# Fp32 value products, and four of six probability blocks turned by transfers and VectorE with one more step of lag, in a transformer block kernel

## The chip, the cores and the metric

The kernel runs on one core of a Trainium2 chip. The core has a matmul engine (TensorE, PE in the rows; its weight loads are PEld), VectorE (DVE), ScalarE (ACT), GpSimd (POOL), a queue engine that issues transfers (SyncE, SP), and 16 DMA engines. The metric is the device time of one execution in microseconds (us). Lower is better.

## The reference

One transformer block is applied to 16 sequences of 256 tokens with 256 channels. Attention has 16 heads of 128 dimensions; all heads share one key and one value projection, and each head scales them per token:

```python
q = (x @ Wq.T).reshape(b, n, H, D)
...
k = jnp.einsum('bnd,bnh->bnhd', kp, kh)
v = jnp.einsum('bnd,bnh->bnhd', vp, vh)
q = rope(q)
k = rope(k)
...
scores = jnp.where(mask[None, None], scores, -jnp.inf)
p = jax.nn.softmax(scores, axis=-1)
o = jnp.einsum('bhnm,bmhd->bnhd', p, v).reshape(b, n, H * D)
return o @ Wout.T
```

The mask is causal. kh and vh come from decayed running sums over the tokens. Layer norms, residual sums and a gated feed-forward part with ternary weights follow. Everything is fp32.

## The kernel before

The attention part handles two heads of one sequence, a pair, at a time: 8 pairs a sequence and 128 pairs in all, numbered g. It is a software pipeline written out by hand. In a step s every engine does one stage of several pairs, in the order written in that engine's `batch` function, and `LAG` says how many steps behind its projection a pair reaches each stage: score 1, softmax 2, turn 3, value 4, out 5. Engines meet only through semaphores. An engine works strictly in its written order, so an instruction that waits holds up all that stands behind it on that engine.

The steps of a pair are:

- TensorE projects its queries (`project`, products of high and low parts: three matmuls for each product). VectorE multiplies by cosines (`queries_cos`), ScalarE swaps halves (`swap`), GpSimd multiplies by sines and adds (`queries_sin`, `queries_add`, lines 616 and 626), and also scales the keys (`scale_keys`, line 639).
- TensorE makes the scores (`score`, lines 950 and 952, plain fp32). For the later 128 queries there are 256 keys, for the earlier 128 queries there are 128: 384 columns, three blocks of 128 x 128 a head, six a pair. VectorE masks them into the SBUF buffer T and finds the maxima (`maxima`, lines 1629 and 1631), ScalarE takes the exponentials (`exponent`), VectorE inverts the sums (`invert_sums`, line 1641), and GpSimd multiplies by the inverses (`normalise`, line 650).
- TensorE turns the six blocks by matmuls with the identity (`turn`, lines 967 to 969). ScalarE scales them by vh and writes the high parts, VectorE the low parts (`split_pt`, line 1654). TensorE multiplies them with the values in three passes (`value`, line 798 with pt_split), and later with Wout (`project_out`, line 798 with wo_hi and wo_lo).

T has two buffers, used by pairs in turn. Once in eight steps there is work for the next sequence (`front_at`) and for the last one (`tail_at`): projections of keys and values, layer norm, the residual sum. In some steps a chunk of the feed-forward weights is made ternary (`weights_...`, VectorE on bf16 tensors in SBUF). SyncE loads the scales of the keys two steps ahead, and moves blocks of 32 columns onto 32 partitions so that VectorE's transpose, which turns squares of 32 x 32, can complete the turn of the next sequence's x (`spread_blocks`, line 490, and `turn_x`, line 1514). The feed-forward part starts in the last steps of attention (`FSTART`, `UNIT0`) and goes on for 16 units.

## Time and profile before

| | |
|---|---|
| time, median of 3 runs | 1030.47 us (1030.17 to 1030.52) |
| profiled execution, its own time | 1030.4 us |
| its span in the profile | 1028.4 us |
| busy: PE, PEld, DVE, ACT, POOL | 1014.0, 975.8, 837.9, 861.1, 911.7 us |
| DMA | 64.19 MB, 62 GB/s in the mean |

The profile is one execution on the chip, taken by the hardware profiler. The span runs from its first instruction to its last; 2.0 us of the execution's own time lie outside. Busy time is the time in which an engine had an instruction under way. Matmuls overlap, so a matmul's duration is longer than the time until the next one starts, and rates are read from the starts.

### The profile page before, as it was taken

To read this page: it belongs to the slowest core of one execution; us is meant where nothing else is said; L and a number is where in the kernel's file an instruction comes from. 1 tells how busy PE (TensorE), PEld (TensorE's weight loads), DVE (VectorE), ACT (ScalarE), POOL (GpSimd) and SP (SyncE) were. 2 spreads that over 40 slices of the span, in tenths; PEclk is the share of its full clock that TensorE was granted. 3 is DMA by queue.
4 is the path that set the end of the run, shared out by engine and by line. 5 is a ranking of instruction groups with operands and counts; after the bars stand their busy time and mean duration, and the time that the engine had idled before them with its cause. 6 is when DMAs were issued, how large, how long until landed. Compare 5 with 4: busy or idle time off the path is not lost. (4 is left out here: it accounts for less than half of the span.)

```text
span 1028.4 us, 25055 instructions
## 1 busy us (share of the span) xinstructions
PE 1014.0 (99%) x7777; PEld 975.8 (95%) x7777; DVE 837.9 (81%) x2871; ACT 861.1 (84%) x2427; POOL 911.7 (89%) x848
## 2 busy tenths in 40 slices
PE   7999999999999999999999999999999999999997
PEld 6899999999999999999999999999999999999997
DVE  6978888888888898889888889887777766677776
ACT  5988888988898989898989898889898867877774
POOL 4888999999999999999999999999899847877786
PEclk9999999999999999999999999999999999999999
DMA  7561121112111211221122112111130000000001
GB/s 255 204 196 48 52 69 52 48 62 69 52 51 61 75 51 53 66 75 48 43 73 78 47 54 77 54 47 64 47 114 33 1 2 12 22 22 28 27 21 42
DMA packets 45587, 64.19 MB, mean 62 GB/s; under 512 B 4512, under 2 KB 26464, under 8 KB 45152
## 3 DMA queue, kind: packets, MB, share of 16 engines
q1 hardware_dynamic: 45456, 62.60, 19.5%
q8 instruction: 62, 1.02, 0.4%
q14 instruction: 69, 0.57, 0.2%
HBM read 50.92 MB, written 9.18 MB: 58 GB/s over the span
## 5 line engine op out<-in xcount | busy, mean ns | idle before, releaser
L650 POOL TENSOR_TENSOR arena<-arena 128x768 f32<-128x768 f32 x128 | 195.9, 1530 | 14.2 <-DVE arena L1641 13.9
L626 POOL TENSOR_TENSOR arena<-arena 128x512 f32<-128x512 f32 x128 | 180.3, 1408 | 10.0
L616 POOL TENSOR_TENSOR arena<-arena,tables 128x512 f32<-128x512 f32 x128 | 165.3, 1292 | 20.0 <-ACT arena L1269 19.3
L1654 DVE SCALAR_TENSOR_TENSOR pt_split<-psum,vh_col,pt_split 128x256 fp32r<-128x256 f32 (+1 forms) x512 | 176.8, 406 | 3.5 <-ACT pt_split L1299 3.4
L639 POOL TENSOR_TENSOR arena<-arena 128x512 f32<-128x512 f32 x127 | 163.3, 1286 | 0.0
L1280 ACT ACTIVATE arena<-arena 128x256 f32<-128x256 f32 x256 | 128.3, 501 | 40.7 <-DVE arena L1631 36.1
L950 PE MATMUL psum<-arena 128*128 128x256 f32 x512 | 153.6, 382 | 3.1 <-POOL arena L626 1.9
L798 PE MATMUL psum<-wo_hi,o_hi 128*128 128x256 f32 x512 | 152.0, 297 | 0.0
L798 PE MATMUL psum<-xt_lo,wq_hi 128*128 128x256 f32 x512 | 144.5, 282 | 0.0
L798 PE MATMUL psum<-xt_hi,wq_lo 128*128 128x256 f32 x512 | 144.4, 282 | 0.0
L798 PE MATMUL psum<-wo_hi,o_lo 128*128 128x256 f32 x512 | 144.2, 282 | 0.0
L798 PE MATMUL psum<-xt_hi,wq_hi 128*128 128x256 f32 x512 | 144.0, 281 | 0.0
L798 PE MATMUL psum<-wo_lo,o_hi 128*128 128x256 f32 x512 | 143.6, 281 | 0.0
L798 PE MATMUL psum<-pt_split,vals_hi 128*128 128x512 f32 (+1 forms) x512 | 142.1, 359 | 0.1
L1038 PE MATMUL psum<-xt_hi,wq_hi 128*128 128x256 f32 x512 | 125.6, 282 | 0.0
L1038 PE MATMUL psum<-xt_lo,wq_hi 128*128 128x256 f32 x512 | 124.4, 284 | 0.0
L1298 ACT ACTIVATE pt_split<-psum,vh_col 128x256 fp32r<-128x256 f32 x256 | 120.6, 471 | 0.4 <-PE psum L969 0.4
L1268 ACT ACTIVATE arena<-psum 64x512 f32<-64x512 f32 x128 | 76.1, 595 | 45.0 <-DVE arena L1616 43.6
L952 PEld LDWEIGHTS psum<-arena 128*128 128x128 f32 x512 | 97.2, 190 | 13.3
L1629 DVE CUSTOM_DVE_ANT_0 arena<-psum,mask 128x256 f32<-128x256 f32 x256 | 106.7, 417 | 0.0
L1663 DVE TENSOR_TENSOR o_lo<-psum,o_hi 128x512 fp32r<-128x512 f32 x128 | 87.1, 680 | 23.6 <-ACT o_hi L1308 23.0
L1282 ACT ACTIVATE arena<-arena 128x128 f32<-128x128 f32 x256 | 99.3, 388 | 0.0
(202 smaller groups left out, 3378.1 us busy)
## 6 DMA issues: line engine op xcount, KB each, us to landing
arena<-kh_rows SPq DMA_DIRECT2D x127, 256.0 KB, 3.4
out<-spare SPq DMA_DIRECT2D x15, 256.0 KB, 2.1
moved<-arena SPq DMA_DIRECT2D x56, 64.0 KB, 2.2
arena<-w_rows SPq DMA_DIRECT2D x6, 512.0 KB, 4.8
X<-L_attn_Wout SPq DMA_DIRECT2D x1, 2048.0 KB, 15.0
X<-L_attn_x SPq DMA_DIRECT2D x1, 2048.0 KB, 9.9
arena<-arena SPq DMA_DIRECT2D x30, 64.0 KB, 2.0
arena<-L_attn_Wq SPq DMA_DIRECT2D x1, 1536.0 KB, 10.6
```

Source lines behind the costliest of these rows:

```text
L616: nc.gpsimd.tensor_tensor(swap, swap, spread, ALU.mult).then_inc(q_sined, 1)
L626: nc.gpsimd.tensor_tensor(q_rot[p % 2], q_cos[p % 2], q_swap[p % 2], ALU.add).then_inc(q_roped, 1)
L639: nc.gpsimd.tensor_tensor(k_head[p % 2], keys[par].unsqueeze(1).to_broadcast([P, HP, N]), kh_all[p % 4], ALU.mult).then_inc(k_scaled, 1)
L650: nc.gpsimd.tensor_tensor(tb, tb, r.unsqueeze(3).to_broadcast([P, HP, 3, P]), ALU.mult).then_inc(p_ready, 1)
L798: last = nc.tensor.matmul(o, a, b, start=start and i == 0, stop=stop and i == len(passes) - 1, skip_group_check=skip)
L950: nc.tensor.matmul(sj[:, 0:2 * P], q[:, j, P:N], kt[:, j, :], start=True, stop=True, skip_group_check=True)
L1038: last = nc.tensor.matmul(bank[c % 2 * 2 + half][:, j * N:(j + 1) * N], wgu_t[:, k, col:col + P], part[:, k, :], start=n == 0 and j == 0, ...
L1280: nc.scalar.activation(tb[:, j, 0:2 * P], tb[:, j, 0:2 * P], ACT.Exp, scale=-1.0, bias=nmax[p % 4][:, 2 * j:2 * j + 1], accum_out=rsum[p % ...
L1282: nc.scalar.activation(tb[:, j, 2 * P:3 * P], tb[:, j, 2 * P:3 * P], ACT.Exp, scale=-1.0, bias=nmax[p % 4][:, 2 * j + 1:2 * j + 2], accum_ ...
L1298: nc.scalar.activation(pt_hi[p % 2][:, j * N:(j + 1) * N], b[:, 0:N], ACT.Copy, scale=vh[:, 0, h:h + 1])
L1629: nc.vector.tensor_tensor_reduce(tb[:, j, 0:2 * P], S_BANK[j][:, 0:2 * P], mask[:, :], -1.0, -MASKED, ALU.add, ALU.min, nmax[p % 4][:, 2 * ...
L1654: last = nc.vector.scalar_tensor_tensor(pt_lo[p % 2][:, o], b[:, i], vh[:, t, h:h + 1], pt_hi[p % 2][:, o].bitcast(F32), ALU.mult, ALU.sub ...
```

## The change

The value products become plain fp32 (two matmuls a pair in place of six), so ScalarE writes the scaled probabilities once, as fp32, and VectorE's low parts go away, as do the low parts of the values. Of the six blocks, TensorE turns only the two of the earlier queries. The four of the later queries are kept in T in another column order (`T_rows`, with the keys of `score` read in that order), moved by four transfers of 64 KB a pair from SyncE (`exchange`), and turned in squares of 32 x 32 by VectorE into the same PSUM banks (`fill_pt`, first in VectorE's step). The stages turn, value and out come one step later, T has three buffers, and the stages of the tail and the start of the feed-forward part are one step later too. `normalise` multiplies 12 groups of 64 columns in place of 6 groups of 128, with inverses written by two reciprocals.

```diff
-LAG = dict(project=0, cos=0, swap=0, key=0, rope=1, score=1, softmax=2, turn=3, value=4, out=5)
+LAG = dict(project=0, cos=0, swap=0, key=0, rope=1, score=1, softmax=2, turn=4, value=5, out=6)
...
-TAIL = dict(copy=5, stats=7, invert=9, norm_a=11, norm_b=12, add=14)
+TAIL = dict(copy=6, stats=8, invert=10, norm_a=12, norm_b=13, add=15)
...
-FSTART = PAIRS + 1
+FSTART = PAIRS + 2
...
+        T_rows = lambda g, j: T[g % 3][:, 0:4 * P].rearrange("p (b j r) -> p b j r", j=HP, r=P // 2)[:, :, j, :]
+        T_early = lambda g, j: T[g % 3][:, (4 + j) * P:(5 + j) * P]
...
+            def exchange(g0, s):
+
+                at = pair_at(g0, s, LAG["softmax"])
+                if at:
+                    g = at[0]
+                    sp.wait_ge(p_ready, g + 1)
+                    at_least(sp, pt_filled, (g - 2) * HP + HP)
+                    for b in range(4):
+                        sp.dma_start(blocks[g % 2][b * 32:(b + 1) * 32, :].rearrange("q (a e) -> q a e", e=P),
+                                     T[g % 3][:, b * P:(b + 1) * P]).then_inc(p_exchanged[g % 2], 16)
...
-                    nc.gpsimd.tensor_tensor(tb, tb, r.unsqueeze(3).to_broadcast([P, HP, 3, P]), ALU.mult).then_inc(p_ready, 1)
+                    nc.gpsimd.tensor_tensor(tb, tb, rinv[p % 4][:, 0:12].unsqueeze(2).to_broadcast([P, 12, P // 2]), ALU.mult)\
+                        .then_inc(p_ready, 1)
...
-                        nc.tensor.matmul(sj[:, 0:2 * P], q[:, j, P:N], kt[:, j, :], start=True, stop=True,
+                        by_blocks = kt[:, j, :].rearrange("p (m b c) -> p b m c", m=NT, b=4)
+                        nc.tensor.matmul(sj[:, 0:2 * P], q[:, j, P:N], by_blocks, start=True, stop=True,
...
-                        b = PT_BANK[j]
-                        at_least(pe, pt_lo_done, head_count(g - 1, j))
-                        nc.tensor.transpose(b[:, 0:P], tb[:, j, 2 * P:3 * P], ident[:, :])
-                        nc.tensor.transpose(b[:, P:2 * P], tb[:, j, 0:P], ident[:, :])
-                        nc.tensor.transpose(b[:, 2 * P:3 * P], tb[:, j, P:2 * P], ident[:, :]).then_inc(pt_ready, 1)
+                        at_least(pe, pt_done, head_count(g - 1, j))
+                        nc.tensor.transpose(PT_BANK[j][:, 0:P], T_early(g, j), ident[:, :]).then_inc(pt_ready, 1)
...
-                    three_passes(O_BANK, [(vh[:, 0, :], vl[:, 0, :], ph[:, first], pl[:, first])], stop=False, skip=True)
-                    three_passes(heads(O_BANK, N)[:, :, P:N], [(vh[:, 1, :], vl[:, 1, :], ph[:, second], pl[:, second])],
-                                 start=False, skip=True).then_inc(o_ready, 1)
+                    nc.tensor.matmul(O_BANK, v[:, 0, :], pv[:, first], start=True, stop=False, skip_group_check=True)
+                    nc.tensor.matmul(heads(O_BANK, N)[:, :, P:N], v[:, 1, :], pv[:, second], start=False, stop=True,
+                                     skip_group_check=True).then_inc(o_ready, 1)
...
-                        act.wait_ge(pt_ready, head_count(g, j))
+                        act.wait_ge(pt_filled, head_count(g, j))
...
-            def split_pt(g0, par, s, j):
+            def fill_pt(g0, s):
 
                 at = pair_at(g0, s, LAG["turn"])
                 if at:
...
+                    g, p, _ = at
+                    dve.wait_ge(p_exchanged[g % 2], g // 2 * 64 + 64)
+                    for j in range(HP):
+                        dve.wait_ge(pt_ready, head_count(g, j))
+                        nc.vector.transpose(PT_BANK[j][:, P:3 * P].rearrange("p (m q a) -> p m a q", m=NT, a=4),
+                                            blocks[g % 2][:, :].rearrange("p (a j m c) -> p j m a c", j=HP, m=NT, c=32)[:, j])\
+                          .then_inc(pt_filled, 1)
```

The order of TensorE's instructions shows turn and value of one step, between the end of `project_out` and the next `project`. Before, from the second head's turn on:

```order
L967 MATMUL psum<-ident,arena 128x128
L968 MATMUL psum<-ident,arena 128x128
L969 MATMUL psum<-ident,arena 128x128
L798 MATMUL psum<-pt_split,vals_hi 128x512 x2
L798 MATMUL psum<-pt_split,vals_lo 128x512
L798 MATMUL psum<-pt_split,vals_hi 128x2x128 x2
L798 MATMUL psum<-pt_split,vals_lo 128x2x128
L798 MATMUL psum<-xt_hi,wq_hi 128x256
```

After the change, both heads' turns and the value products of the same place:

```order
L817 MATMUL psum<-wo_hi,o_lo 128x256
L985 MATMUL psum<-ident,arena 128x128 x2
L1000 MATMUL psum<-pt,vals 128x512
L1001 MATMUL psum<-pt,vals 128x2x128
L817 MATMUL psum<-xt_hi,wq_hi 128x256
```

Six turns became two, and six value matmuls became two, one of 512 and one of 256 columns.

VectorE's order at the fifth step of a sequence (`L1556` or `L1572` are the decays of the next sequence, `BN_STATS` its statistics). Before:

```order
L1631 ISA arena 128x1
L1556 RECIPROCAL psum<-arena 32x128
L1641 RECIPROCAL arena<-arena 128x8
L1500 BN_STATS arena<-X 128x6
L1505 BN_AGGR arena<-arena 128x2 x2
L1663 TENSOR_TENSOR o_lo<-psum,o_hi 128x512
L1616 TENSOR_TENSOR arena<-psum,tables 128x512
L1654 SCALAR_TENSOR_TENSOR pt_split<-psum,vh_col,pt_split 128x256
L1654 SCALAR_TENSOR_TENSOR pt_split<-psum,vh_col,pt_split 128x128
```

After the change:

```order
L1642 ISA arena 128x1
L1666 STREAM_TRANSPOSE psum<-blocks 128x2x4x32 x2
L1572 RECIPROCAL psum<-arena 32x128
L1653 RECIPROCAL inverses<-arena 128x8
L1655 RECIPROCAL inverses<-arena 128x4
L1516 BN_STATS arena<-X 128x6
L1521 BN_AGGR arena<-arena 128x2 x2
L1675 TENSOR_TENSOR o_lo<-psum,o_hi 128x512
L1625 TENSOR_TENSOR arena<-psum,tables 128x512
L1639 MEMSET arena 128x1
```

The four low parts (L1654) behind the cosines are gone, and two transposes stand ahead of everything else in the step.

SyncE's order around the same sequence's last steps, before and after:

```order
L483 DMA arena<-kh_rows 128x512 x2
L490 DMA moved<-arena 32x4x128 x4
L535 DMA w_tern_t<-arena 128x512
L483 DMA arena<-kh_rows 128x512 x4
```

```order
L499 DMA blocks<-T_third 32x4x128 x4
L488 DMA arena<-kh_rows 128x512
L506 DMA moved<-arena 32x4x128 x4
L551 DMA w_tern_t<-arena 128x512
L499 DMA blocks<-arena 32x4x128 x4
L488 DMA arena<-kh_rows 128x512
```

Between any two loads of key scales (L483, now L488) there are now four transfers of blocks (L499), which wait for `normalise`.

## Rows read from the trace of the kernel before

**Rows 1.** The page, part 1: busy us and share of the span

```profile
PE 1014.0 (99%) x7777; PEld 975.8 (95%) x7777; DVE 837.9 (81%) x2871; ACT 861.1 (84%) x2427; POOL 911.7 (89%) x848
```

**Rows 2.** Windows: stretch, length, busy us (instructions) per engine, granted clock, DMA share, GB/s

```profile
412.00:512.00 100.00, 100.00 (x757) 95.81 (x755) 87.62 (x320) 88.45 (x269) 95.39 (x80) 1.00 0.19 60
712.00:805.00 93.00, 93.00 (x706) 89.27 (x705) 70.85 (x284) 81.46 (x245) 85.14 (x72) 1.00 0.19 62
```

**Rows 3.** Timeline of PE in one step: start us, duration us, engine, line, operation

```profile
500.72 0.27 PE L967 MATMUL psum<-ident,arena 128*128 128x128 f32 x1
...
501.26 0.27 PE L969 MATMUL psum<-ident,arena 128*128 128x128 f32 x1
...
502.43 0.28 PE L798 MATMUL psum<-xt_hi,wq_hi 128*128 128x256 f32 x1
...
503.87 0.59 PE L950 MATMUL psum<-arena 128*128 128x256 f32 x2
...
504.52 0.38 PE L950 MATMUL psum<-arena 128*128 128x256 f32 x1
```

**Rows 4.** Timeline of PE: the first turn in two steps that follow each other

```profile
432.57 0.27 PE L967 MATMUL psum<-ident,arena 128*128 128x128 f32 x1
...
438.44 0.27 PE L967 MATMUL psum<-ident,arena 128*128 128x128 f32 x1
```

**Rows 5.** Timeline of POOL in three steps

```profile
413.61 1.27 POOL L616 TENSOR_TENSOR arena<-arena,tables 128x512 f32<-128x512 f32 x1
...
418.88 1.30 POOL L616 TENSOR_TENSOR arena<-arena,tables 128x512 f32<-128x512 f32 x1
...
421.62 2.35 POOL L650 TENSOR_TENSOR arena<-arena 128x768 f32<-128x768 f32 x1
...
429.65 1.47 POOL L650 TENSOR_TENSOR arena<-arena 128x768 f32<-128x768 f32 x1
```

**Rows 6.** Groups of POOL, 413 to 513.2: busy us, mean ns | idle before, releaser

```profile
L650 POOL TENSOR_TENSOR arena<-arena 128x768 f32<-128x768 f32 x16 | 24.8, 1552 | 1.2 <-DVE arena L1641 1.2
...
L616 POOL TENSOR_TENSOR arena<-arena,tables 128x512 f32<-128x512 f32 x16 | 20.6, 1286 | 1.3 <-ACT arena L1269 1.3
...
L607 POOL TENSOR_TENSOR X<-X,arena 128x512 f32<-128x512 f32 x2 | 2.6, 1288 | 0.0
```

**Rows 7.** Timelines of DVE and POOL at two places

```profile
421.46 1.18 DVE L1688 TENSOR_TENSOR arena<-arena 128x1024 bf16<-128x1024 bf16 x1
...
714.08 0.73 DVE L1514 STREAM_TRANSPOSE psum<-moved 128x512 f32<-128x512 f32 x1
714.34 1.29 POOL L626 TENSOR_TENSOR arena<-arena 128x512 f32<-128x512 f32 x1
```

**Rows 8.** Timeline from one pair's scores to the next pair's

```profile
435.71 0.59 PE L950 MATMUL psum<-arena 128*128 128x256 f32 x2
...
437.24 0.59 ACT L1269 ACTIVATE arena<-psum 64x512 f32<-64x512 f32 x1
...
438.56 0.51 ACT L1280 ACTIVATE arena<-arena 128x256 f32<-128x256 f32 x1
...
439.27 1.29 POOL L626 TENSOR_TENSOR arena<-arena 128x512 f32<-128x512 f32 x1
...
440.46 0.20 DVE L1641 RECIPROCAL arena<-arena 128x8 f32<-128x8 f32 x1 [0.56 <-ACT arena L1282]
...
441.61 0.38 PE L950 MATMUL psum<-arena 128*128 128x256 f32 x1
```

**Rows 9.** Groups of DVE, whole span, columns as in rows 6

```profile
L1654 DVE SCALAR_TENSOR_TENSOR pt_split<-psum,vh_col,pt_split 128x256 fp32r<-128x256 f32 (+1 forms) x512 | 176.8, 406 | 3.5 <-ACT pt_split L1299 3.4
```

**Rows 10.** SyncE's timeline: four issues of 64 KB, merged

```profile
407.11 2.54 SPq L490 DMA_DIRECT2D moved<-arena  x4
```

**Rows 11.** The tile `moved`: its 56 transfers of 64 KB each

```profile
DMA to landing us min/median/max: 2.2/2.2/3.9
```

**Rows 12.** Waits of PE, whole span: waiting line, releaser, us, times, longest

```profile
PE psum L950 <- POOL arena L626: 1.9, 3, 0.9
```

More of the change, by code:

```diff
@@ L54 @@
 FRONT = dict(move=-1, turn=0, split=0, split_lo=1, keys=1, gates=2, gates_one=2, key_cos=3, key_swap=3, key_rope=4,
-             decay_a=3, decay_b=4, coef=5, weigh=5, sum=5, store=6, made=5, taken=5, turned=6, values_hi=7, values_lo=7, vh=7)
+             decay_a=3, decay_b=4, coef=5, weigh=5, sum=5, store=6, made=5, taken=5, turned=6, values_copy=7, vh=7)
 AHEAD = dict(stats_a=3, stats_b=4, invert=5, norm_a=6, norm_b=6, move=7)
@@ L67 @@
 FLEAD = 8
-UNIT0 = dict(stats=-4, invert=-3, norm_a=-2, norm_b=-1, turn=0, split=0, split_lo=1, up=PAIRS + 1, multiply=PAIRS + 2)
-FSTART = PAIRS + 1
+UNIT0 = dict(stats=-4, invert=-3, norm_a=-2, norm_b=-1, turn=0, split=0, split_lo=1, up=PAIRS + 2, multiply=PAIRS + 3)
+FSTART = PAIRS + 2
 FC = 2
@@ L110, in sandwich_kernel @@
         moved = sb("moved", [P, NT * E])
+        blocks = [sb(f"blocks{i}", [P, 4 * P]) for i in range(2)]
+        inverses = sb("inverses", [P, 64])
+        T_third = sb("T_third", [P, HP * 3 * P])
         cosq, sinq, cosk, sink = (tables[:, i, :] for i in range(4))
@@ L115, in sandwich_kernel @@
         xt_lo = [sb(f"xt_lo{i}", [P, ET, N], F32R) for i in range(2)]
-        vals_hi = [sb(f"vals_hi{i}", [P, NT, D], F32R) for i in range(2)]
-        vals_lo = [sb(f"vals_lo{i}", [P, NT, D], F32R) for i in range(2)]
+        vals = [sb(f"vals{i}", [P, NT, D]) for i in range(2)]
         vh_col = [sb(f"vh_col{i}", [P, NT, 2 * H]) for i in range(2)]
@@ L125, in sandwich_kernel @@
         spare = sb("spare", [P, 2 * NT * E])
-        pt_split = sb("pt_split", [P, 2, 2, 6 * P], F32R)
-        pt_hi, pt_lo = ([pt_split[:, j, i, :] for i in range(2)] for j in range(2))
+        pt_all = sb("pt", [P, 2, 6 * P])
+        pt = [pt_all[:, i, :] for i in range(2)]
         arena = sb("arena", [P, ARENA])
@@ L148, in sandwich_kernel @@
         T_at = used[0]
-        T = [carve(HP, 3 * P) for _ in range(2)]
+        T = [carve(HP * 3 * P) for _ in range(2)] + [T_third[:, :]]
         k_head = [carve(HP, N) for _ in range(2)]
@@ L210, in sandwich_kernel @@
         rsum = [small[:, 16 + 4 * i:20 + 4 * i] for i in range(4)]
-        rinv = [small[:, 96 + 8 * i:104 + 8 * i] for i in range(4)]
+        rinv = [inverses[:, 16 * i:16 * i + 16] for i in range(4)]
         ln1_stat = small[:, 48:60].rearrange("p (t a) -> p t a", a=6)
@@ L535, in batch @@
                         sp.dma_start(rows.rearrange("(p f) -> p f", f=FF // 2), w_turned_bf).then_inc(wt_stored, 16)
+                    exchange(g0, s)
             store_kh(0, 0)
@@ L1640, in invert_sums @@
                     dve.wait_ge(p_exp, head_count(g, HP - 1))
-                    nc.vector.reciprocal(heads(rinv[p % 4], 2), rsum[p % 4].unsqueeze(2).to_broadcast([P, 2 * HP, 2]))\
-                        .then_inc(p_inv, 1)
-            def split_pt(g0, par, s, j):
+                    sums, made = rsum[p % 4].rearrange("p (j t) -> p t j", t=NT), rinv[p % 4]
+                    nc.vector.reciprocal(made[:, 0:8].rearrange("p (b j) -> p b j", j=HP),
+                                         sums[:, 0, :].unsqueeze(1).to_broadcast([P, 4, HP]))
+                    nc.vector.reciprocal(made[:, 8:12].rearrange("p (j h) -> p j h", j=HP),
+                                         sums[:, 1, :].unsqueeze(2).to_broadcast([P, HP, 2])).then_inc(p_inv, 1)
+            def fill_pt(g0, s):
                 at = pair_at(g0, s, LAG["turn"])
                 if at:
-                    g, p, back = at
-                    vh, h, b = vh_col[par ^ back], H + p * HP + j, PT_BANK[j]
-                    dve.wait_ge(pt_hi_done, head_count(g, j))
-                    at_least(dve, o_ready, g - 1)
-                    for t, (o, i) in enumerate(((slice(j * N, (j + 1) * N), slice(0, N)),
-                                                (slice(HP * N + j * P, HP * N + (j + 1) * P), slice(N, N + P)))):
-                        last = nc.vector.scalar_tensor_tensor(pt_lo[p % 2][:, o], b[:, i], vh[:, t, h:h + 1],
-                                                              pt_hi[p % 2][:, o].bitcast(F32), ALU.mult, ALU.subtract)
-                    last.then_inc(pt_lo_done, 1)
+                    g, p, _ = at
[5 more added lines that the diff above has]
+                          .then_inc(pt_filled, 1)
             def split_o(g0, s):
@@ L1934, in batch @@
                         queries_cos(g0, s)
-                    for j in range(HP):
-                        split_pt(g0, par, s, j)
                     if g0 == STEPS:
```

93 lines of the change are left out of this document (44 added, 49 removed).

## The prediction

> **What bounds the kernel now.** I read the busy times first. TensorE is busy for 99% of the span, GpSimd for 89% [rows 1]. The windows place this: between 412 and 512 us TensorE has no idle time and its weight loads are busy for 95.8 of 100 us, at a granted clock of 1.00, and GpSimd is busy for 95.4 [rows 2]. So in attention, which is some 780 us of the span, TensorE ends everything last. From 712 us, when the ternary chunks are done, GpSimd has 85.1 of 93. The list of waits agrees: TensorE waited for GpSimd's add for only 1.9 us in all [rows 12].
>
> How near GpSimd is decides this case. A regular step is 5.87 us long on TensorE [rows 4], and GpSimd's four instructions of a step repeat after 5.27 (413.61 to 418.88) [rows 5]. The other steps are longer on both, and 16 steps, two sequences, take 100.2 us, the length of the window that rows 6 come from. In these 16 steps GpSimd waited for another engine for 1.2 us ahead of `normalise` and 1.3 ahead of the sines [rows 6]. It therefore needs about 100.2 - 2.5 = 97.7 us for its own work. That is all the room there is below TensorE.
>
> Part of this need is not work. At 421.62 `normalise` took 2.35 us in place of 1.47 [rows 5], while VectorE ran a bf16 comparison with two inputs in SBUF from 421.46 on for 1.18 [rows 7]. There are six such VectorE instructions in 16 steps, as long as chunks are made.
>
> **The change part by part.**
>
> Turns: the first starts at 500.72, the sixth at 501.26, so they follow at 0.11 us each [rows 3], though each lasts 0.27. Four fewer: 4 x 0.11 = 0.44 us a step less.
>
> Here a rule is weighed that would change the term. The Trainium skill ("TensorE: Matmul & The Clock Gate", PE-mode transpose) gives about 275 ns for a transpose of 128 x 128 inside a kernel. The trace has the same 0.27 us as a duration, but not as the distance of starts. By the page's figure the term would be about 1.1 us; by the starts it is 0.44.
>
> Values: before, from the end of the last turn (501.26 + 0.11) to the first projection at 502.43 are 1.06 us [rows 3]. Plain fp32 is in the scores: from 503.87 to 504.52 are 0.65 us for 256 + 128 columns [rows 3], 1.69 ns a column. 768 columns give 1.30 us, 0.24 more. A column of fp32 in the scores costs the same in both sizes, so I take this as it is, with 0.05 us either way.
>
> TensorE's step becomes 5.87 - 0.44 + 0.24 = 5.67, by 0.20 shorter with rounding; I use 0.19. If only TensorE mattered: 128 x 0.19 = 24.3 us less.
>
> VectorE: it loses 4 x 0.406 us of low parts a step [rows 9] and gets two transposes and a second reciprocal. The transpose of 512 columns took 0.73 [rows 7]; half of it costs between 0.37 and about 0.45 if part is fixed, so 0.9 for two, plus 0.20 [rows 8]: 1.1 against 1.62. Hidden, and VectorE gets freer. The transposes now stand first in its step and wait for TensorE's turns; queued behind them are `invert_sums`, the weights' work, and what GpSimd needs of them. In rows 8 the scores start at 435.71 and the next turns at 438.44 [rows 4], 2.73 later. The transposes would end about 2.73 + 0.2 + 0.9 = 3.85 after the scores' start. The exponentials of the pair started at 438.56 and the sums were inverted at 440.46, 1.90 later [rows 8]. Without the low parts ahead of the maxima they can start when the swap is done at 437.83, 2.12 after the scores' start, so they end at about 4.05. The add of GpSimd, ahead of `normalise`, ends at 440.56, 4.85 after [rows 8]. So the transposes are covered by 0.2 us at one point and a microsecond at the other. Without the cover, each late 0.1 us would first eat into that microsecond.
>
> Do the new transposes hold up GpSimd, as the bf16 comparison did? At 714.08 the existing one ran for 0.73 beside the add of 714.34, which took its usual 1.29 [rows 7]. I cost it at nothing.
>
> Transfers: four issues take SyncE 2.54 us [rows 10], and with one landing in 2.2 us the last arrives 1.9 + 2.2 = 4.1 us after `normalise`; at the longest landing of 3.9 [rows 11] it is 5.8. `normalise` at 429.65 ended at 431.12 [rows 5] and its turn started at 432.57 [rows 4]: 1.45. With one step more of lag the room is 1.45 + 5.68 = 7.1. Hidden by 1.3 to 3.0. SyncE issues for 2.54 + about 0.4 of 6.1 us, and the key scales, loaded two steps ahead, stand behind.
>
> `normalise`: the same 768 columns in 12 groups. Below: nothing. Above: 768 columns in six groups take 1.47 [rows 5], 512 columns in two groups 1.29 [rows 6]; if the 256 further columns were free, the groups would cost 0.18, and twice as many 0.18 again. But 256 columns are not free at 1.29 for 512, so I take 0.
>
> What GpSimd gives back. While chunks are made (96 of 128 steps), TensorE would want 100.2 - 16 x 0.19 = 97.2 us for 16 steps and GpSimd 97.7. The slack that evens this out is short: the add ends at 440.56, the scores that need it start at 441.61 [rows 8], 1.05 us; with the shorter step it is 0.86. I carried GpSimd's lag from step to step through 16 steps, with its extra work in the steps where the new `TAIL` puts it. The residual sum of 1.29 [rows 6] moves from the seventh to the eighth step, where the weights' scales also stand. It reaches 1.2 us three times, and TensorE waits 0.8 to 1.6 us in 16 steps. I take 1.2, times 6 = 7.2. As GpSimd no longer idles, VectorE's bf16 instructions hit it more fully. The one in rows 5 cost it 0.88. Over 16 steps `normalise` lost 16 x (1.552 - 1.47) = 1.3 us to them [rows 6], so by far not all six cost as much today. I add 0.5 for 16 steps, 3.0, as an estimate between 0 and 2 a period. In the other 32 steps it needs its 85.1 plus some 2 of gaps of its own (estimate, 97.7 - 95.4 for 16 steps in the busier stretch), 87.2, against 93 - 15 x 0.19 = 90.1: no wait.
>
> Start and drain: one more step of turn, value and out (0.22 + 1.30 + 1.43 = 2.95 us of TensorE) moves from the filling of the pipeline, where TensorE has idle time, to its emptying, where pairs now pass through transfers and VectorE too. I take 2.0, between 0 and 4.
>
> Sum on the profiled execution: 1030.4 - 24.3 + 7.2 + 3.0 + 2.0 = 1018.3. It lies at the median of the runs, 1030.47, so 1018 for the median. The forecast is faster by 12 us, half of what TensorE saves, GpSimd the new bound for three quarters of attention.
>
> **The rivals.**
>
> Full gain: GpSimd's collisions and waits are absorbed, since VectorE is freer and delivers its sums earlier. For it: VectorE's load falls by half a microsecond a step. Against it: the 97.7 us. It gives 1030.4 - 24.3 + 2 to 5 = 1008 to 1011. Chance 0.12.
>
> GpSimd dearer, which ends on the other side: `normalise` over 12 groups costs more, or collisions come in full. Place: the 96 steps with 97.7 of 97.2 us, where each 0.1 us goes wholly into the time, 9.6 us, and less in the other 32 with their 0.2 us of room a step. It decides from about 0.12 us a step. At the upper bound of 0.18 it gives 1018 + 96 x 0.18 = 1035, and 1037 with some waits in the other 32. For it: no row has this shape. Against: the price by column. Chance 0.25, with 0.06 still faster, 0.06 the same and 0.13 slower.
>
> Here the Trainium skill ("SBUF — State Buffer", Who interferes with whom) states that a VectorE instruction with two SBUF inputs and a reading GpSimd instruction exclude each other for the whole instruction. Rows 5 and 7 agree: 0.88 us more beside an instruction of 1.18. By the rule in full, each of the six would cost 1.18, 0.3 more than here: 1.8 in 16 steps, 11 us in all, 1026 in place of the 1018 that counts 3.0 of it.
>
> Late blocks: the exchange takes over 7.1 us, VectorE stands at the head of its step, and its sums, low parts and cosines are late with it. For it: SyncE waits in order for chunk stores and layer norms. Against: 4.1 to 5.8. With 7.5 us, 0.4 a step: 1018 + 128 x 0.4 less the overlap with GpSimd's waits, about 1050. Chance 0.05.
>
> Dear turns: the distance of starts understates what four turns cost, and TensorE's step falls by 1.1 - 0.24. Then GpSimd alone bounds: 6 x (100.2 - 97.7) + 2 x (93.0 - 87.2) = 27 us, and with 2 for start and drain 1005. It is what the page's figure would do. Chance 0.02.
>
> **How the numbers follow.** Forecast 0.56 for 1011 to 1025. With the others: faster by over 0.2% (about what a measurement of this kernel can tell from no change) 0.56 + 0.12 + 0.06 + 0.02 = 0.76, the same 0.06, slower 0.13 + 0.05 = 0.18. The range of 1008 to 1033 leaves out half of the full gain's low side, the dear turns, and the slower cases beyond a few microseconds, 0.2 together.
>
> **What the next profile would show.** TensorE's turn to first projection 1.52 us apart, down from 1.71. Regular steps of 5.68. `normalise` at 1.47 when undisturbed. GpSimd's idle ahead of `normalise` and the sines near zero between 412 and 512, and TensorE waiting 1 to 2 us for the add in 16 steps. 16 steps in 98 to 99 us. VectorE's transposes at 0.37 to 0.45, with waits for TensorE but none for transfers, and landings of 2.2. The prediction is wrong if `normalise` is longer, if VectorE waits for the transfers, or if the scores' rate changes with the new order of the keys, which I cost at nothing.

## The result and the profile after

The changed kernel takes 1044.81 us (median of 4 runs, 1042.77 to 1046.26) against 1030.32 us (1030.13 to 1030.52) before on the same chip. The ratio is 1.0139, 95% interval 1.0125 to 1.0154. It is slower by 14.5 us, where 12 us less were forecast. The profiled execution took 1044.94 us and its span is 1042.8, so here too some 2 us lie outside.

The page of the changed kernel, part 1, answers to [rows 1]:

```profile
PE 1003.8 (96%) x7009; PEld 906.7 (87%) x7009; DVE 759.0 (73%) x2727; ACT 855.5 (82%) x2427; POOL 903.3 (87%) x849
```

TensorE lost 10 us of busy time and the span gained 14, so it now has idle time that it did not have. The windows say the same, against [rows 2]:

```profile
412.00:512.00 100.00, 96.83 (x639) 85.23 (x638) 74.48 (x288) 84.72 (x262) 91.53 (x77) 0.98 0.33 98
712.00:805.00 93.00, 92.85 (x623) 81.69 (x622) 63.94 (x271) 83.32 (x257) 87.54 (x75) 1.00 0.39 113
```

The row to look at is GpSimd's: 91.5 of 100 us where it was 95.4. The prediction said that GpSimd would become the bound, and it is idler than before. Something has to be late for it. Rows from the list of waits of the changed kernel (waiting line, releaser, us, times, longest):

```profile
DVE psum L1666 <- PE psum L985: 111.3, 122, 2.7
ACT arena L1284 <- DVE arena L1625: 75.6, 91, 3.8
PEld psum L970 <- POOL arena L645: 32.1, 35, 2.4
POOL arena L668 <- DVE inverses L1655: 29.3, 34, 3.4
...
PE psum L970 <- POOL arena L645: 24.0, 20, 2.2
...
POOL T_third L668 <- DVE inverses L1655: 11.3, 14, 1.4
...
DVE psum L1666 <- DMA blocks<-T_third: 4.4, 1, 4.4
```

TensorE's wait for GpSimd's add was 1.9 us [rows 12] and is 24.0. VectorE now stands for 111.3 us at the head of its step, waiting for TensorE's turns; ScalarE's swap waits 75.6 us for the cosines. GpSimd waits for the inverses for 29.3 and 11.3 us (two rows, by T's buffer), where it was 13.9 before. For transfers there is a single wait of 4.4 us, so they are hidden, as was said.

**Where the time went.** I took the start of each pair's first score matmul from TensorE's timelines and cut the span with it: the first 16 steps with what is ahead of them, the 96 steps with chunks of weights, the last 15 steps, and from the last pair's scores to the end. In us:

| | before | after | change | predicted |
|---|---|---|---|---|
| to the scores of pair 16 | 121.6 | 122.0 | +0.4 | -3.0 |
| 96 steps | 601.4 | 612.0 | +10.6 | -8.0 |
| last 15 steps | 91.4 | 89.7 | -1.7 | -2.9 |
| from the last scores on | 214.0 | 219.0 | +5.0 | +2.0 |
| span | 1028.4 | 1042.8 | +14.4 | -11.9 |

The column "predicted" splits the prediction's sum: 0.19 us less a step everywhere, +7.2 and +3.0 in the 96 steps, +2.0 for start and drain put in the last row, and the last pair's own 0.2 left out. So 18.6 of the 26 us of error are in the 96 steps.

**What happens there.** The waits of GpSimd alone in the 96 steps, before and then after:

```profile
POOL arena L616 <- ACT arena L1269: 8.7, 26, 0.7
POOL arena L650 <- DVE arena L1641: 6.9, 25, 0.6
```

```profile
POOL arena L668 <- DVE inverses L1655: 20.4, 26, 1.4
POOL T_third L668 <- DVE inverses L1655: 9.2, 12, 1.4
POOL arena L635 <- ACT arena L1285: 4.3, 12, 0.5
```

GpSimd was idle for 15.6 us in them and is now for 33.9, and the added time is nearly all ahead of `normalise` (29.6 us in place of 6.9). There are 38 such waits. In 21 of them, 19.5 us together, the exponentials had ended 1.3 to 3.0 us before the inversion started, and the inversion was queued on VectorE behind the transposes and the work that follows them. In the other 17, 10.0 us, the inversion waited for the exponentials on ScalarE. Steps are counted from a sequence's first, in twos of sequences. The first kind stands in the second, third, ninth and eleventh of 16 steps, the second in the eighth and the last two. In the kernel before the inversion came 0.03 us after the exponentials' end in most steps, and 0.8 at most in the mean of a step's place. Here is the first kind, in a second step of 16:

```profile
427.27 0.19 ACT L1298 ACTIVATION_READ_ACCUMULATOR arena<-arena 128x1 f32 x1
...
427.85 0.79 DVE L1666 STREAM_TRANSPOSE psum<-blocks 128x256 f32<-128x256 f32 x2 [1.42 <-PE psum L985]
428.55 0.67 DVE L1534 TENSOR_TENSOR xt_lo<-psum,xt_hi 128x512 fp32r<-128x512 f32 x1
429.14 0.17 DVE L1653 RECIPROCAL inverses<-arena 128x8 f32<-128x8 f32 x1
...
429.44 2.36 POOL L668 TENSOR_TENSOR arena<-arena,inverses 128x768 f32<-128x768 f32 x1 [1.22 <-DVE inverses L1655]
```

The longest waits of TensorE, 1.8 us, come behind the last of 16 steps. Its rows, from the timelines of PE, DVE, ACT and POOL of the changed kernel (start, duration, engine, line, operation):

```profile
412.14 0.79 DVE L1666 STREAM_TRANSPOSE psum<-blocks 128x256 f32<-128x256 f32 x2 [0.24 <-PE psum L985]
...
413.03 0.49 ACT L1296 ACTIVATE arena<-arena 128x256 f32<-128x256 f32 x1
...
414.78 0.70 PE L970 MATMUL psum<-arena 128*128 128x256 f32 x2
...
414.91 0.20 DVE L1653 RECIPROCAL inverses<-arena 128x8 f32<-128x8 f32 x1 [1.99 <-ACT arena L1298]
...
415.05 0.57 ACT L1324 ACTIVATE o_hi<-psum 128x512 fp32r<-128x512 f32 x1
...
415.23 1.47 POOL L668 TENSOR_TENSOR arena<-arena,inverses 128x768 f32<-128x768 f32 x1 [0.51 <-DVE inverses L1655]
...
415.65 0.69 DVE L1675 TENSOR_TENSOR o_lo<-psum,o_hi 128x512 fp32r<-128x512 f32 x1
...
416.26 0.68 DVE L1625 TENSOR_TENSOR arena<-psum,tables 128x512 f32<-128x512 f32 x1
...
417.92 1.28 POOL L626 TENSOR_TENSOR X<-X,arena 128x512 f32<-128x512 f32 x1
419.29 0.27 POOL L676 TENSOR_SCALAR arena<-arena 128x16 bf16<-128x16 f32 x1
...
420.34 1.28 POOL L635 TENSOR_TENSOR arena<-arena,tables 128x512 f32<-128x512 f32 x1
421.70 1.27 POOL L645 TENSOR_TENSOR arena<-arena 128x512 f32<-128x512 f32 x1
...
423.02 1.02 PE L970 MATMUL psum<-arena 128*128 128x256 f32 x2 [1.81 <-POOL arena L645]
```

Two things meet. The cosines (L1625) start 1.48 us after the scores' start, though TensorE has their input ready by then. In the kernel before they start 0.20 us after it in 11 of the 16 steps that I laid side by side, and never later than 0.8. At this place the transposes are not what holds them: they ended at 412.93, and VectorE then stood for 1.99 us until ScalarE had the exponentials. ScalarE had been busy with the swap, held up by the cosines of the step before (410.09), with a layer norm, and with the exponentials, and it writes the high part of o (L1324) behind them, for which the low part (L1675) and the cosines wait. So a late cosine comes back one step later through ScalarE as late sums and a late cosine. The second thing is GpSimd's queue: after waits of 0.69, 0.50 and 0.51 us in three instructions it is busy without a pause from 415.23 to 422.97, with the residual sum (L626) and the weights' scales (L676 to 679) in one step. The sines (L635) start 2.16 us after the swap's end at 418.18, and TensorE idles for 1.81. In the eighth step of the 16 there is a second such place with 1.2 us of idle time.

### The profile page after: what moved, and what is told of

Read it like the earlier page. It is cut to its first block and busy times, and to the rows that moved or that the text cites. A ratio compares the mean times of both kernels' runs of the same rounds, so it can differ in the third digit from the quotient of the medians.

```text
span 1042.8 us, 23874 instructions
## 1 busy us (share of the span) xinstructions
PE 1003.8 (96%) x7009; PEld 906.7 (87%) x7009; DVE 759.0 (73%) x2727; ACT 855.5 (82%) x2427; POOL 903.3 (87%) x849
## 5 line engine op out<-in xcount | busy, mean ns | idle before, releaser
L970 PE MATMUL psum<-arena 128*128 128x256 f32 x512 | 160.6, 396 | 25.6 <-POOL arena L645 24.0
L1666 DVE STREAM_TRANSPOSE psum<-blocks 128x256 f32<-128x256 f32 x256 | 100.7, 439 | 115.7 <-PE psum L985 111.3
L645 POOL TENSOR_TENSOR arena<-arena 128x512 f32<-128x512 f32 x128 | 171.3, 1338 | 10.0
L635 POOL TENSOR_TENSOR arena<-arena,tables 128x512 f32<-128x512 f32 x128 | 164.4, 1284 | 10.0 <-ACT arena L1285 9.1
L817 PE MATMUL psum<-xt_hi,wq_hi 128*128 128x256 f32 x512 | 167.8, 328 | 0.2 <-ACT arena L1285 0.2
L658 POOL TENSOR_TENSOR arena<-arena 128x512 f32<-128x512 f32 x127 | 163.6, 1289 | 0.0
L668 POOL TENSOR_TENSOR arena<-arena,inverses 128x768 f32<-128x768 f32 x86 | 132.2, 1538 | 29.9 <-DVE inverses L1655 29.3
L1284 ACT ACTIVATE arena<-psum 64x512 f32<-64x512 f32 x128 | 76.2, 595 | 79.9 <-DVE arena L1625 75.6
L1000 PE MATMUL psum<-pt,vals 128*128 128x512 f32 x256 | 131.2, 594 | 1.5 <-DVE o_lo L1675 1.5
L1054 PE MATMUL psum<-xt_hi,wq_hi 128*128 128x256 f32 x512 | 125.6, 282 | 0.0
L1314 ACT ACTIVATE pt<-psum,vh_col 128x256 f32<-128x256 f32 x256 | 120.3, 470 | 4.2 <-DVE psum L1666 4.2
L972 PEld LDWEIGHTS psum<-arena 128*128 128x128 f32 x512 | 98.8, 193 | 14.1
L970 PEld LDWEIGHTS psum<-arena 128*128 128x128 f32 x512 | 78.3, 192 | 34.3 <-POOL arena L645 32.1
L1675 DVE TENSOR_TENSOR o_lo<-psum,o_hi 128x512 fp32r<-128x512 f32 x128 | 86.6, 676 | 27.9 <-ACT o_hi L1324 26.0
L1001 PEld LDWEIGHTS psum<-pt,vals 128*128 128x128 f32 x256 | 48.6, 190 | 61.2 <-issue 61.2
L817 PEld LDWEIGHTS psum<-xt_hi,wq_hi 128*128 128x128 f32 x512 | 96.5, 188 | 4.2 <-issue 0.9
## 6 DMA issues: line engine op xcount, KB each, us to landing
X<-L_attn_x SPq DMA_DIRECT2D x1, 2048.0 KB, 11.3
```

The lines of the kernel that those rows point to most:

```text
L635: nc.gpsimd.tensor_tensor(swap, swap, spread, ALU.mult).then_inc(q_sined, 1)
L645: nc.gpsimd.tensor_tensor(q_rot[p % 2], q_cos[p % 2], q_swap[p % 2], ALU.add).then_inc(q_roped, 1)
L658: nc.gpsimd.tensor_tensor(k_head[p % 2], keys[par].unsqueeze(1).to_broadcast([P, HP, N]), kh_all[p % 4], ALU.mult).then_inc(k_scaled, 1)
L668: nc.gpsimd.tensor_tensor(tb, tb, rinv[p % 4][:, 0:12].unsqueeze(2).to_broadcast([P, 12, P // 2]), ALU.mult)\
L817: last = nc.tensor.matmul(o, a, b, start=start and i == 0, stop=stop and i == len(passes) - 1, skip_group_check=skip)
L970: nc.tensor.matmul(sj[:, 0:2 * P], q[:, j, P:N], by_blocks, start=True, stop=True, skip_group_check=True)
```

## The experiments

In the expectations, theory A is that the inverses of the sums come late and hold up `normalise`; theory B that the bunching of residual sum and scales costs the time; theory D that the cosines come late on VectorE; C and E are told in the expectations themselves. Every kernel is compared with the kernel before. The mean of the six 16-step stretches of the 96 steps, from the timelines, stands beside each: it is 100.2 us before and 102.0 after.

**fill_late.** The two transposes go behind the inversion of the sums.

```diff
-                    fill_pt(g0, s)
...
                     invert_sums(g0, s)
+                    fill_pt(g0, s)
```

> The changed kernel with VectorE's transposes of a step behind the inversion of the sums instead of first in the step. Theory A (the transposes wait for TensorE's turns at the head of VectorE's step, the inverses are late behind them, and GpSimd, which has no room, stands idle ahead of normalise for 5.8 us in 16 steps): GpSimd's idle there falls to about 1 us, 16 steps fall from 103.1 to 99 or 100 us, and the time to 1020 to 1027. Theory B (the residual sum and the weights' scales now meet in one step and only that stalls TensorE): the time stays within 3 us of 1044.8. Theory C (transfers and SyncE's longer queue slow the steps): no change either.

Measured: 1051.29 us (1050.88 to 1053.34), ratio 1.0208 (1.0191 to 1.0225), 6.5 us more than the change, and 16 steps in 102.9. Its waits:

```profile
DVE inverses L1653 <- ACT arena L1298: 98.6, 74, 3.0
...
POOL arena L635 <- ACT arena L1285: 30.6, 44, 4.3
ACT pt L1314 <- DVE psum L1666: 25.7, 39, 4.2
...
POOL arena L668 <- DVE inverses L1655: 12.2, 18, 1.7
```

GpSimd's wait for the inverses fell from 29.3 to 12.2 us and the time still grew, so the 1020 to 1027 of theory A fail. VectorE now stands waiting for the sums of the exponentials, and what is behind, transposes and cosines, is later still: ScalarE's write of pt waits 25.7 us for the transposes, and the sines 30.6 for the swap. It doesn't show that late inverses are harmless. In the 96 steps GpSimd's waits for them fall from 29.6 to 12.6 us and those for the swap rise from 4.3 to 18.6: this edit moves the idle time from one path to the other.

**add14.** The residual sum goes back to the seventh step.

```diff
-TAIL = dict(copy=6, stats=8, invert=10, norm_a=12, norm_b=13, add=15)
+TAIL = dict(copy=6, stats=8, invert=10, norm_a=12, norm_b=13, add=14)
```

> The changed kernel with the residual sum one step earlier (TAIL add=14), so that it does not meet the weights' scales. Theory B: the wait of TensorE of some 2 us in the last step of every second sequence goes, with the clock's drop behind it, 10 to 13 us in all: 1032 to 1035. Theory A: GpSimd still idles ahead of normalise, and only some of that wait goes: 1038 to 1043. Theory C: no change.

Measured: 1034.99 us (1032.17 to 1035.58), 1.0041 (1.0027 to 1.0055), 9.8 us less than the change, 16 steps in 100.0. Theory B holds: one digit is worth 9.8 us. In the 96 steps no wait of TensorE for the add is over 1.0 us any more.

**fill_late_add14.** Both edits together.

> Both edits. Theory A with B as a smaller second part: 1016 to 1022, what the sum of the prediction said. If either alone gives all, this equals that one within 2 us.

Measured: 1046.31 us (1045.48 to 1047.12), 1.0157 (1.0140 to 1.0174), 16 steps in 101.9, where 1016 to 1022 was expected: a miss, for the reason seen in fill_late. The late transposes cost 11.3 us beside add14, more than the 6.5 beside the change: with the bunched step out of the way less of them lies under another wait, as I read it.

**turn_early.** TensorE makes the two turns right behind the scores of the step before, so that VectorE finds them done. (In the fourth step of the first sequence, where a later turn of weights uses the place, they come at the step's end.)

```diff
-                    turn(g0, par, s)
                     value(g0, par, s)
...
                     score(g0, par, s)
...
+                    else:
+                        turn(g0, par, s + 1)
...
+                    if is_first(g0, s - 3):
+                        turn(g0, par, s + 1)
```

> The changed kernel with VectorE's order as it is, but TensorE's two turns of a pair right behind the scores of the step before, ahead of the next sequence's work and the output products. Theory A in its narrow form (what costs is the wait for the turn, not the 0.9 us that the transposes take at the head of the step): as good as fill_late or better, 1018 to 1027, and VectorE's wait for the turns of 111 us goes below 30. If the transposes' own time ahead of the inverses costs: 1030 to 1038. Theories B and C: within 3 us of 1044.8.

Measured: 1036.72 us (1035.59 to 1037.80), 1.0061 (1.0044 to 1.0078), 8.1 us less than the change, 16 steps in 100.6. The row of VectorE's 111.3 us of waits for the turns is gone from the list, and GpSimd's waits for the inverses in the 96 steps fall from 29.6 to 10.5 us. So the path through the inverses does cost. The 1018 to 1027 for the wait alone failed; the run lies in the 1030 to 1038 that was expected if the transposes' own time costs too.

**fill_small.** Each transpose turns a single square of 32 columns in place of 256; most of the turning is left out.

```diff
-                        nc.vector.transpose(PT_BANK[j][:, P:3 * P].rearrange("p (m q a) -> p m a q", m=NT, a=4),
-                                            blocks[g % 2][:, :].rearrange("p (a j m c) -> p j m a c", j=HP, m=NT, c=32)[:, j])\
+                        nc.vector.transpose(PT_BANK[j][:, P:P + 32], blocks[g % 2][:, j * 32:(j + 1) * 32])\
```

> The changed kernel, in which each of VectorE's two transposes of a pair turns one square column of 32 instead of all 256 columns, at the same place and with the same waits. It leaves out most of the turning, so the probabilities of the later queries are not right. Theory D, formed after the first four runs (the cosines of the queries come late, because the transposes, the inversion and the low part of the output all have to pass through VectorE between TensorE's turns and the end of its projection, and the sines, the add and the scores are late behind them): the transposes' own 0.9 us falls to some 0.4, cosines start 0.2 us after the scores' start in most steps again, and the time falls by 8 to 14 us to 1031 to 1037. If only the wait for the turns mattered: within 3 us of 1044.8.

Measured: 1037.57 us (1037.08 to 1038.67), 1.0069 (1.0052 to 1.0086), 7.2 us less, 16 steps in 101.3. The transposes' own length costs about as much as their wait for the turns, though only 4.3 of the 7.2 us are in the 96 steps and 2.0 are up to pair 16. Neither is hidden.

**cos_first.** On VectorE the cosines go ahead of the low part of o. Two calls change places.

```diff
-                    if g0 < STEPS:
-                        split_o(g0, s)
                     if not (is_first(g0, s) or is_first(g0, s - 2) or is_first(g0, s - 3)):
                         queries_cos(g0, s)
+                    if g0 < STEPS:
+                        split_o(g0, s)
```

> The changed kernel with the cosines ahead of the low part of the output on VectorE. Theory D: 0.67 us leave the path to the cosines: the time falls by 5 to 12 us, to 1033 to 1040, and 16 steps take 100.5 to 101.5 us. If the low part of the output is what TensorE then waits for in its value products, the time does not fall.

Measured: 1033.56 us (1031.58 to 1036.69), 1.0034 (1.0022 to 1.0046), 11.3 us less than the change, the most of any single edit, with 16 steps in 100.2. Its waits:

```profile
DVE arena L1625 <- PE psum L817: 48.0, 62, 1.9
ACT arena L1284 <- DVE arena L1625: 47.4, 107, 3.8
```

The first row does not exist in the changed kernel's list. Here VectorE comes to its cosines before TensorE's queries are done and waits for them 62 times. ScalarE's wait for the cosines is 47.4 us, down from 75.6 and near the 43.6 that the same wait has in the trace before. GpSimd's waits in the 96 steps fall for the swap from 4.3 to 2.1 us and for the inverses from 29.6 to 20.1, the latter, as I read it, since the swap stands ahead of the exponentials on ScalarE: the 17 waits for them, 10.0 us, become 6 with 2.9. Theory D holds, and its path goes through the sums too.

**te_add14.** turn_early and add14 together.

> The changed kernel with the turns early and the residual sum one step earlier. By theory D with the bunching of GpSimd's extra work as a second cause, both give their parts (8 and 10 us): 1025 to 1029, 16 steps in 99 to 99.5 us. If they are one cause: 1034 to 1037.

Measured: 1029.88 us (1026.77 to 1031.09), 0.9989 (0.9979 to 0.9998), 16 steps in 99.2.

**te_add14_cos.** The three edits that helped, together.

> The same and the cosines ahead of the low part of the output. Theory D: 1 to 4 us less than the kernel without it, 1022 to 1027, 16 steps near GpSimd's own need of 97.7 to 98.5 us. If GpSimd alone bounds by now: no change.

Measured: 1024.28 us (1023.98 to 1025.76) beside 1030.24 for the kernel before, ratio 0.9942 (0.9925 to 0.9958). It beats both kernels, and is 5.6 us below te_add14, where 1 to 4 were expected. Its window:

```profile
412.00:512.00 100.00, 99.57 (x670) 87.57 (x669) 78.67 (x304) 89.18 (x273) 96.78 (x81) 1.00 0.36 103
```

TensorE is back at 99.6 and GpSimd is at 96.8, above the 95.4 of [rows 2]. 16 steps take 98.7 us; the prediction had 98 to 99. In the 96 steps GpSimd waits for others for 6.7 us only, which leaves 97.6 us of its own for 16 steps, where the prediction had 97.7. So its picture of GpSimd as the new bound fits this kernel, and was wrong for the one that it was made for. No run made GpSimd's own work cheaper, so that it bounds here is read from the trace and not shown by an edit.

**cos_first_add14.** The last kernel with the turns where the change has them.

> The changed kernel with the residual sum back at the seventh step and the cosines ahead of o_lo, but the turns where the change has them. Theory D (late cosines and the bunched residual sum are all of the loss in the chunk steps): both gains together are limited by TensorE's step; the 16-step periods come to 99.0 to 99.6 and the time to 1027 to 1030. Theory E (the turns standing late on TensorE hold up VectorE and cost more by themselves): the version with early turns and these two edits, at 1024.3, is the better one by 3 us or more, with periods of 98.8 against 99.4 or more here. If the early turns add nothing, this one is at 1023 to 1025 too.

Measured: 1027.61 us (1026.93 to 1033.08), 0.9977 (0.9964 to 0.9990), 16 steps in 99.4. The early turns are worth about 3 us beside the other two edits, as theory E had it; alone they were worth 8.1. The gains of the single edits do not add up (11.3 + 9.8 + 8.1 = 29.2, together 20.5), since they all shorten the same chain.

**before_fp32.** The kernel before, with only the value products in plain fp32. TensorE turns all six blocks, and nothing is moved.

```diff
-                    three_passes(O_BANK, [(vh[:, 0, :], vl[:, 0, :], ph[:, first], pl[:, first])], stop=False, skip=True)
-                    three_passes(heads(O_BANK, N)[:, :, P:N], [(vh[:, 1, :], vl[:, 1, :], ph[:, second], pl[:, second])],
-                                 start=False, skip=True).then_inc(o_ready, 1)
+                    nc.tensor.matmul(O_BANK, v[:, 0, :], pv[:, first], start=True, stop=False, skip_group_check=True)
+                    nc.tensor.matmul(heads(O_BANK, N)[:, :, P:N], v[:, 1, :], pv[:, second], start=False, stop=True,
+                                     skip_group_check=True).then_inc(o_ready, 1)
...
-                    for j in range(HP):
-                        split_pt(g0, par, s, j)
```

> The kernel before with only the value products in plain fp32: one copy of values and of scaled probabilities, two value matmuls a pair in place of six, no low parts on VectorE; TensorE still turns six blocks, no transfers, the lag as before. By the prediction's term TensorE's step gets 0.24 us longer (0.20 to 0.29), times 128 = 26 to 37 us: 1056 to 1067, periods of 16 steps of 104.0, and TensorE waits for nobody. Rival: fp32 value matmuls cost what the scores cost a column only beside other fp32 work; then the step grows by another amount and the distance from the last turn to the first projection shows it (predicted 1.30 plus 0.11).

Measured: 1055.83 us (1055.67 to 1056.88), 1.0245 (1.0228 to 1.0263), 25.3 us more, just below the lower end. TensorE is busy for all of the window from 412 to 512. A regular step is 6.11 us long in place of 5.87 [rows 4]: the 0.24 of the prediction, to the digit. 16 steps take 103.8. By stretches it is +1.7 up to pair 16, +21.0 in the 96 steps, +2.3 in the last 15 and +0.6 behind them. So 2.1 of the 5.4 us that are missing to 30.7 are at the start, where TensorE has idle time, 2.0 in the 96 steps, where steps with other work grow by less than 0.24 (6.51 to 6.70, 7.31 to 7.54), and 1.3 in the last 15. TensorE's timeline at the same place as [rows 3]:

```profile
503.11 0.27 PE L968 MATMUL psum<-ident,arena 128*128 128x128 f32 x1
503.21 1.02 PE L983 MATMUL psum<-pt,vals 128*128 128x512 f32 x2
504.08 0.59 PE L984 MATMUL psum<-pt,vals 128*128 128x256 f32 x2
504.32 0.47 PE L797 MATMUL psum<-xt_hi,wq_hi 128*128 128x256 f32 x1
504.63 0.28 PE L797 MATMUL psum<-xt_lo,wq_hi 128*128 128x256 f32 x1
504.75 0.28 PE L797 MATMUL psum<-xt_hi,wq_lo 128*128 128x256 f32 x1
```

From the first value product to the first projection are only 1.11 us. The other 0.19 are behind the first projection, which is followed after 0.31 us where the next ones follow after 0.12. Together they are the 1.30 of the prediction.

**before_fp32_lag.** The same with one step more of lag and three buffers of T. The tail and the start of the feed-forward part come one step later too, but the residual sum stays at its step.

```diff
-LAG = dict(project=0, cos=0, swap=0, key=0, rope=1, score=1, softmax=2, turn=3, value=4, out=5)
+LAG = dict(project=0, cos=0, swap=0, key=0, rope=1, score=1, softmax=2, turn=4, value=5, out=6)
...
-TAIL = dict(copy=5, stats=7, invert=9, norm_a=11, norm_b=12, add=14)
+TAIL = dict(copy=6, stats=8, invert=10, norm_a=12, norm_b=13, add=14)
...
-FSTART = PAIRS + 1
+FSTART = PAIRS + 2
...
-        T = [carve(HP, 3 * P) for _ in range(2)]
+        T = [carve(HP, 3 * P) for _ in range(2)] + [T_third[:, :].rearrange("p (a b) -> p a b", b=3 * P)]
```

> The same kernel with turn, value and out one step later, T in three buffers, and the tail and the start of the feed-forward part one step later, but the residual sum left at its step. The turns still stand on TensorE. The prediction's term for start and drain alone: 0 to 4 us more than the kernel without the lag, all of it after the last steps of attention, with the 16-step periods unchanged within 0.2. The other theory, that the lag itself (not the transfers or VectorE's transposes) costs the 5 us that the change lost after the last scores: +5, with TensorE's idle time after the last scores about 2 us. If the lag costs nothing there, the drain's loss belongs to the transfers and transposes.

Measured: 1059.18 us (1058.75 to 1059.71), 1.0275 (1.0258 to 1.0292), 3.35 us more than before_fp32. The 16-step stretches are the same, 103.8. From the last scores on it is 4.7 us longer (219.3 against 214.6), and 1.2 are won up to pair 16. So the lag alone makes about as much as the 5.0 us that the changed kernel lost at its end. What transfers and transposes add there is not split off: TensorE's idle time grows by 0.8 us here and by 1.7 in the changed kernel, whose moved work is smaller.

## Why the prediction was wrong

1. TensorE's step: right. In the changed kernel the turn starts at 188.44 and the first projection at 189.76, 1.32 later; the next one follows after 0.30 in place of 0.12, so again 0.18 lie behind it. That makes 1.50 against the 1.52 forecast. Regular steps take 5.68, as said. before_fp32 gives the value term by itself, 6.11 - 5.87 = 0.24. So TensorE's own need fell as forecast, by 24.3 us.

```profile
188.44 0.38 PE L985 MATMUL psum<-ident,arena 128*128 128x128 f32 x2
188.66 1.02 PE L1000 MATMUL psum<-pt,vals 128*128 128x512 f32 x2
189.51 0.59 PE L1001 MATMUL psum<-pt,vals 128*128 128x256 f32 x2
189.76 0.47 PE L817 MATMUL psum<-xt_hi,wq_hi 128*128 128x256 f32 x1
190.06 0.28 PE L817 MATMUL psum<-xt_lo,wq_hi 128*128 128x256 f32 x1
```

2. VectorE, "Hidden, and VectorE gets freer": **this step failed**, on two paths. The price of a transpose was right (mean 439 ns, group row below, against 0.37 to 0.45), and freer VectorE is (759 us against 838). The first path goes through the inverses to `normalise`. I read its cover of 0.2 us and a microsecond from one regular step [rows 8], and in regular steps it holds, GpSimd is not idle there. In the steps with work for the next sequence or on a chunk it does not: there the inverses come out of VectorE's queue 1.3 to 3.0 us after the exponentials' end, and GpSimd, which had no room, idles for 19.5 us in 21 of the 96 steps. turn_early takes 8.1 us off and fill_small 7.2. The second path I did not follow at all. The cosines are queued behind the same transposes in the order rows that I had shown myself, and their path (swap, sines, add, scores, and the swap on ScalarE ahead of the next exponentials) has a slack of 1.05 us. They became 0.2 to 0.9 us later in most steps, behind the transposes, and up to 1.3 in the last ones of 16, there by way of ScalarE. cos_first takes 11.3 us off by a swap of two calls. Busy time fell by 79 us and lateness rose: a share of busy time says nothing of when an instruction starts.

```profile
L668 POOL TENSOR_TENSOR arena<-arena,inverses 128x768 f32<-128x768 f32 x86 | 132.2, 1538 | 29.9 <-DVE inverses L1655 29.3
...
L1666 DVE STREAM_TRANSPOSE psum<-blocks 128x256 f32<-128x256 f32 x256 | 100.7, 439 | 115.7 <-PE psum L985 111.3 <-DMA blocks<-T_third 4.4
```

3. GpSimd's lag, +7.2: mis-sized for this kernel, where TensorE waits 18.5 us for the add in the 96 steps. The residual sum in the step of the scales was named and carried in the sum, but with the inverses and the cosines on time. Late cosines and the two jobs come together to 1.81 us of idle time in the last of 16 steps and 1.2 in the eighth. add14 measures 9.8 us for the bunching alone. In te_add14_cos, with both out of the way, the 96 steps take 9.1 us less than before, where the prediction has 8.0 less. Its +3.0 for dearer collisions shows nowhere: GpSimd's own need for 16 steps is 97.6 us there, the same as 97.6 in the kernel before by the same count. Nor do the 11 us of collisions in full.

4. GpSimd dearer (the rival with the chance of 0.25, the larger of the two on the slower side): no. `normalise` over 12 groups takes 1538 ns in the mean over the whole span (group row above) against 1530 in the same view of the kernel before, and 1.47 us when it runs undisturbed, as in [rows 5]. The kernel landed on that rival's side, and beyond its 1037, for another reason. The rival late blocks had the right mechanism in its second half, sums and cosines late with the head of VectorE's step, but for the transfers as the cause and only at 0.05. I had both halves in hand and joined them only for that case.

5. Transfers: hidden. The tile `blocks` has the median landing that was forecast; its longest of 9.6 us gives the one wait of 4.4:

```profile
DMA to landing us min/median/max: 2.1/2.2/9.6
```

6. Start and drain, +2.0 between 0 and 4: mis-sized. The lag measured by itself costs 3.35. The work of 2.95 us does move to the emptying, with 1.7 us of idle time of TensorE on top (7.4 against 5.7 after the last scores). At the start it left idle time behind (10.6 against 7.7 us up to pair 16), so the first 16 steps won nothing though their steps are shorter. Even the best kernel has +0.8 and +4.9 in these two rows of the table, where -3.0 and +2.0 were forecast: 6.7 us, which is more than its distance of 6.0 from the predicted 1018.3.

7. The price of a turn: the Trainium skill's 275 ns ("TensorE: Matmul & The Clock Gate", PE-mode transpose) would have made four turns worth 1.1 us. The step of 5.68 settles it: 5.87 + 0.24 - 0.44 = 5.67, and with 1.1 it would be 5.01. As a duration the figure agrees with the rows, 0.27 us.

What stays open: how much of the excess in the 96 steps belongs to each of the three (the turns' wait, the transposes, the order of the low part) can't be split, as their gains overlap; and I did not try any other place for the transposes than the two shown, above all not one behind the cosines.

## What to carry to other kernels

An instruction that waits at the head of an in-order engine's step delays everything behind it. List each consumer behind it, and check the slack of each path to the bounding engine; the cover found on one path says nothing of the next. Check it in the steps with extra work, and not only in a regular one. Either let the instructions of the shortest slack go ahead, or make the input of the added work earlier; whether the added work itself is better placed behind them was not tried here. Two swapped calls, one digit of a stage table and an earlier turn are worth 20.5 us, and turn a loss of 14 into a gain of 6. When all stages are moved by one step, look again at which jobs now share a step, and count what one more step costs at the end by itself.

## What the runs showed of the hardware

In two places of the 96 steps of the changed kernel TensorE's granted clock fell after it had been idle for 1.81 us: at 218.14 and at 423.02, where the row of two score matmuls shows 1.02 us (above) and is else 0.59 to 0.70. Windows at the second place, columns as in the windows above, the third from the right is the clock:

```profile
423.00:424.00 1.00, 0.98 (x3) 0.81 (x4) 0.00 (x0) 0.99 (x2) 1.00 (x1) 0.63 0.43 122
424.00:426.00 2.00, 2.00 (x10) 1.82 (x9) 0.89 (x7) 1.19 (x4) 2.00 (x3) 0.50 0.60 153
426.00:427.00 1.00, 1.00 (x7) 1.00 (x7) 0.43 (x4) 0.93 (x6) 0.92 (x2) 0.66 0.36 103
```

A clock of 0.50 is the 1.2 GHz level. The step took 7.39 us against 5.76 for the same one of the next 16, so one drop costs 1.6 us, and these two are why two of the six stretches have 103.5 and 103.4 us and the others at most 101.8. After idle times of 1.80, 1.81 and 1.78 us at 321.20, 526.38 and 628.22 the clock stayed at 1.00. After the shorter waits of 1.0 to 1.3 us in turn_early and cos_first the scores behind them kept their usual length. Near the start of cos_first_add14, after 2.11 us of waiting for the add up to 51.52, the clock is 0.60 in the microsecond from 52 and 0.50 from 53 to 56. In turn_early it was idle for 1.52 us up to 820.44, and the clock is 0.53 in the microsecond from 821 and 0.50 from 822 to 824, while six idle times of 1.54 to 1.70 us in the 96 steps of fill_late left it at 1.00. Idle time of TensorE of 1.5 us and more can thus cost as much again, but does not always.

A second one: plain fp32 matmuls reach into what follows. Behind the last fp32 value product the first projection lasts 0.47 us and is followed after 0.31, where its neighbours last 0.28 and follow after 0.12. Who reads only the starts up to the next line's first instruction misses 0.19 of 1.30 us.
